# Folding two blocks of a random-feature projection at a time, each head on half the rows of TensorE's array

## The reference

```python
q = split_heads(x @ Wq.T + bq)          # 16 heads of 64
k = split_heads(x @ Wk.T + bk)
v = split_heads(x @ Wv.T + bv)
q_prime = relu(einsum('bhsd,hmd->bhsm', q, P)) / sqrt(64)   # P: 16 heads, 64 x 64
k_prime = relu(einsum('bhsd,hmd->bhsm', k, P)) / sqrt(64)
kv   = einsum('bhsm,bhsd->bhmd', k_prime, v)
attn = einsum('bhsm,bhmd->bhsd', q_prime, kv)
return attn @ Wo.T + bo
```

## Time and profile before

| | us |
|---|---|
| median of 3 runs | 1084.22 |
| lowest, highest | 1081.37, 1086.16 |
| the profiled execution | 1083.93 |
| its span | 1082.2 |
| TensorE products, busy | 1063.5 |
| TensorE weight loads, busy | 882.9 |
| VectorE, ScalarE, GpSimd, busy | 536.0, 289.8, 349.7 |

### The profile page before, as it was taken

The page is one execution under the profiler, slowest core; times in us unless marked ns, Lnnn a source line. Parts: engine busy times, 40 slices in busy tenths (PEclk is TensorE's granted clock), DMA queues, the critical chain, the costliest instruction groups (busy, mean ns, idle before and its releaser), DMA issues.

```text
span 1082.2 us, 15217 instructions
## 1 busy us (share of the span) xinstructions
PE 1063.5 (98%) x5527; PEld 882.9 (82%) x5527; DVE 536.0 (50%) x1152; ACT 289.8 (27%) x445; POOL 349.7 (32%) x225
## 2 busy tenths in 40 slices
PE   8999999999999999999969999999999999999998
PEld 7887778887878888888858888887788888888887
DVE  6944666676641222132427657967325212214684
ACT  5320211112222234132222223267222212202221
POOL 4000011122230024385400249955108744500151
PEclk9999999999999999999989999999999999999999
DMA  7303011222233387735594557766045556205912
GB/s 270 98 30 108 13 35 52 63 69 72 69 122 88 139 309 245 260 127 185 178 330 182 204 189 217 197 170 181 1 161 196 206 180 218 64 24 227 375 66 110
DMA packets 135933, 163.17 MB, mean 151 GB/s; under 512 B 8534, under 2 KB 102578, under 8 KB 130738
## 3 DMA queue, kind: packets, MB, share of 16 engines
q1 hardware_dynamic: 135282, 160.33, 44.8%
q10 hardware_dynamic: 576, 1.84, 0.4%
HBM read 107.70 MB, written 54.45 MB: 150 GB/s over the span
## 4 chain that ended last, share of the span: by engine, by line
PE 85%; DMA 5%; DVE 3%; POOL 3%; SPq 2%; ACT 1%; issue 1%; ACTq 0%; POOLq 0%
PE ps L2225 7%; PE ps L2227 7%; PE ps L2226 7%; PE ps L1890 6%; PE ps L1892 6%; PE ps L1891 6%; PE ps L2136 6%; PE ps L2138 6%; PE ps L2137 6%; PE ps L2159 4%; PE ps L2165 4%; PE ps L2056 3%; PE ps L2057 3%; PE ps L2058 3%; PE ps L1900 2%; PE ps L2002 2%
## 5 line engine op out<-in xcount | busy, mean ns | idle before, releaser
L1890 PE MATMUL ps<-w_hi,xnH 128*128 128x512 f32 x464 | 184.6, 398 | 0.0
L1892 PE MATMUL ps<-w_hi,xnL 128*128 128x512 f32 x464 | 180.9, 390 | 0.0
L1891 PE MATMUL ps<-w_lo,xnH 128*128 128x512 f32 x464 | 180.7, 389 | 0.0
L892 POOL TENSOR_TENSOR acc<-acc,cw 128x320 f32<-128x320 f32 x40 | 35.7, 893 | 252.6 <-ACT cw L1096 251.4
L1892 PEld LDWEIGHTS ps<-w_hi,xnL 128*128 128x128 f32 x464 | 87.1, 188 | 18.6
L1890 PEld LDWEIGHTS ps<-w_hi,xnH 128*128 128x128 f32 x464 | 87.1, 188 | 18.6
L1891 PEld LDWEIGHTS ps<-w_lo,xnH 128*128 128x128 f32 x464 | 87.2, 188 | 17.2
L1841 DVE TENSOR_TENSOR prd<-ps,wB 128x512 f32<-128x512 f32 (+1 forms) x24 | 14.2, 592 | 141.7 <-PE ps L2227 102.2
L2056 PE MATMUL ps<-xnH,w_hi 128*128 128x512 f32 (+1 forms) x192 | 68.1, 355 | 0.0
L2225 PE MATMUL ps<-x2H,guH 128*128 128x512 f32 (+1 forms) x192 | 67.7, 352 | 0.4 <-ACT wT L1334 0.4
L2226 PE MATMUL ps<-x2L,guH 128*128 128x512 f32 (+1 forms) x192 | 67.6, 352 | 0.0
(11 more groups left out here) (474 smaller groups left out, 2245.8 us busy)
## 6 DMA issues: line engine op xcount, KB each, us to landing
cR<-c_d SPq DMA_DIRECT2D x20, 640.0 KB, 4.8
foldin<-in SPq DMA_DIRECT2D x32, 256.0 KB, 2.8
guR<-in SPq DMA_DIRECT2D x16, 512.0 KB, 6.7
w_raw<-in SPq DMA_DIRECT2D x14, 512.0 KB, 6.6
c_d<-cw SPq DMA_DIRECT2D x40, 160.0 KB
wdq<-in SPq DMA_DIRECT2D x6, 1024.0 KB, 8.0
qR<-qT_d SPq DMA_DIRECT2D x20, 256.0 KB, 4.7
wd_d<-wd1H SPq DMA_DIRECT2D x5, 1024.0 KB, 5.4
```

The source lines that it names most:

```text
L1890: pe.matmul(target, xnH[:, kc, cols], wH[w][:, kc, :], start=(kc == 0), stop=False)
L1891: pe.matmul(target, xnH[:, kc, cols], wL[w][:, kc, :], start=False, stop=False)
L1892: mm = pe.matmul(target, xnL[:, kc, cols], wH[w][:, kc, :], start=False, stop=(kc == KC - 1))
```

## The change

Folds are made in pairs kc, kc + 1, in steps 2, 4, 6 and 8 of the stages (in the q stage after q jobs 1, 3, 5 and 7). A pair uses both `foldin` buffers. Each product takes one head: 64 rows of `foldin` (128 columns) against the 64 by 64 block of P without its zeros, at `tile_position=(a * HD, 0)`. The even heads (a = 0, rows 0 to 63) of both blocks go to the bank of the first job, the odd ones (rows 64 to 127) to the bank of the second. Even and odd products alternate. ScalarE and VectorE read a bank per job as before and put it, by head, in the two blocks' places of the panel. Both jobs are complete with the last products of the pair. `load_fold` and its place in SyncE's queue are as before.

```diff
+FOLD_AT = (2, 4, 6, 8)
@@ _job_ids
             names.append(("v", hf, t))
-            if 1 <= t <= KC:
-                names.append(("fold", hf, t - 1))
+            if t in FOLD_AT:
+                names += [("fold", hf, t - 2), ("fold", hf, t - 1)]
         for t in range(NT):
             names.append(("k", hf, t))
-            if hf == 1 and 1 <= t <= KC:
-                names.append(("fold", 2, t - 1))
+            if hf == 1 and t in FOLD_AT:
+                names += [("fold", 2, t - 2), ("fold", 2, t - 1)]
     for j in range(24):
         names.append(("q", j))
-        names.append(("fold", 3, j) if j < KC else ("m", (j - KC) // 2, (j - KC) % 2))
+        if j >= KC:
+            names.append(("m", (j - KC) // 2, (j - KC) % 2))
+        elif j % 2:
+            names += [("fold", 3, j - 1), ("fold", 3, j)]
@@
+        def by_heads(panel, kc):
+            rows = panel[:, kc - kc % 2:kc - kc % 2 + 2, :].rearrange("q k (g a m) -> q a k g m", g=4, a=2)
+            return rows[:, kc % 2]
+
+        def two_rows(target):
+            return target.rearrange("q (k g m) -> q k g m", k=2, g=4)
@@ fold_high
-                act.activation(wH[(1, 1, 0, 1)[f]][:, kc, :], job_bank(name), ACT.Copy).then_inc(fold_hi, 1)
+                act.activation(by_heads(wH[(1, 1, 0, 1)[f]], kc), two_rows(job_bank(name)), ACT.Copy).then_inc(fold_hi, 1)
@@ fold_low
-                dve.tensor_tensor(wL[w][:, kc, :], job_bank(name), wH[w][:, kc, :].bitcast(F32), ALU.subtract)\
+                dve.tensor_tensor(by_heads(wL[w], kc), two_rows(job_bank(name)), by_heads(wH[w], kc).bitcast(F32), ALU.subtract)\
                    .then_inc(ev, 1)
@@ ScalarE, VectorE and TensorE, each stage (the first shown)
-                if 1 <= t <= KC:
-                    fold_low(0, t - 1)
+                if t in FOLD_AT:
+                    for kc in (t - 2, t - 1):
+                        fold_low(0, kc)
...
-                if 1 <= t <= KC:
-                    fold(0, t - 1)
+                if t in FOLD_AT:
+                    fold(0, t - 2)
@@ fold on TensorE
-                name, n = ("fold", f, kc), fold_index(f, kc)
-                free_bank(name)
-                pe.wait_ge(in_fold[n % 2], 16 * (n // 2 + 1))
-                for g in range(4):
-                    mm = pe.matmul(job_bank(name)[:, g * P:(g + 1) * P], foldin[:, n % 2, g, :],
-                                   pbd_s[:, f % 2 * 4 + g, :], start=True, stop=True)
-                mm.then_inc(mm_done, 1)
+                names = (("fold", f, kc), ("fold", f, kc + 1))
+                for name in names:
+                    n = fold_index(f, name[2])
+                    free_bank(name)
+                    pe.wait_ge(in_fold[n % 2], 16 * (n // 2 + 1))
+                for k in range(2):
+                    for g in range(4):
+                        for a, name in enumerate(names):
+                            half = slice(a * HD, (a + 1) * HD)
+                            mm = pe.matmul(two_rows(job_bank(name))[:, k, g, :], foldin[half, k, g, :],
+                                           pbd_s[half, f % 2 * 4 + g, half], start=True, stop=True,
+                                           tile_position=(a * HD, 0))
+                            if k == 1 and g == 3:
+                                mm.then_inc(mm_done, 1)
```

More of the change, by code:

```diff
@@ L1087, in _ @@
                     act.activation(fbr[:], bank(5)[0:KC, P:2 * P], ACT.Copy).then_inc(bias_ev, 1)
-                if 1 <= t <= KC:
-                    fold_high(0, t - 1)
+                if t in FOLD_AT:
+                    for kc in (t - 2, t - 1):
+                        fold_high(0, kc)
             def window_out(w):
@@ L1106, in _ @@
                     panel_hi(0, t - 4, 2)
-                if s >= 2 * NT and 1 <= t <= KC:
-                    fold_high(s // NT - 1, t - 1)
+                if s >= 2 * NT and t in FOLD_AT:
+                    for kc in (t - 2, t - 1):
+                        fold_high(s // NT - 1, kc)
                 for w in WINDOWS.get(s, ()):
@@ L1153, in _ @@
                 q_feature(j)
-                if j < KC:
-                    fold_high(3, j)
-                else:
+                if j < KC and j % 2:
+                    for kc in (j - 1, j):
+                        fold_high(3, kc)
+                elif j >= KC:
                     g, h = (j - KC) // 2, (j - KC) % 2
@@ L1579, in _ @@
                     v_out(1, t)
-                if s >= 2 * NT and 1 <= t <= KC:
-                    fold_low(s // NT - 1, t - 1)
+                if s >= 2 * NT and t in FOLD_AT:
+                    for kc in (t - 2, t - 1):
+                        fold_low(s // NT - 1, kc)
             def m_low(g, h):
@@ L1594, in _ @@
             for j in range(24):
-                if j < KC:
-                    fold_low(3, j)
-                else:
+                if j < KC and j % 2:
+                    for kc in (j - 1, j):
+                        fold_low(3, kc)
+                elif j >= KC:
                     m_low((j - KC) // 2, (j - KC) % 2)
@@ L2038, in _ @@
                     rows(("v", hf, t), t, 0, ready=4 if t == 0 else None)
-                if s >= 2 * NT and 1 <= t <= KC:
-                    fold(s // NT - 1, t - 1)
+                if s >= 2 * NT and t in FOLD_AT:
+                    fold(s // NT - 1, t - 2)
                 for portion in PORTIONS.get(s, ()):
@@ L2085, in _ @@
                     degrees()
-                if j < KC:
-                    fold(3, j)
-                else:
+                if j < KC and j % 2:
+                    fold(3, j - 1)
+                elif j >= KC:
                     mixed((j - KC) // 2, (j - KC) % 2)
```

## The result

The changed kernel takes 1097.62 us (median; 1095.95 to 1100.98) where the kernel before takes 1085.00 beside it: a ratio of 1.0129 (95% interval 1.0114 to 1.0144), some 13 to 14 us slower. The forecast was +6.3 us, 1090.5. The direction was right and so was the price of the tiles, but the size was half of what came: more than half of the loss arose at a place where the prediction had put nothing. The profiled execution's span went from 1082.2 to 1095.7 us, +13.5.

What follows compares the result with a forecast made beforehand. TensorE's queue was taken to set the time. Steady part 0, tiling overhead 5.0, bank order 0.8 and x9's load 0.5 summed to +6.3 us, 1090.5 us against the median; own range 1087 to 1094, wider range 1083 to 1120.

Steps and rivals of the forecast that it cites:

- the price of the tiles: Sixteen fold pairs on TensorE: coming and going between tilings costs 0.29 or 0.35 us a pair, 5.0 us in all.
- The steady part is worth nothing: Fold pairs on TensorE: row halves load side by side, 1.79 us a pair, the same as two folds now.
- The serial rival: Fold pairs on TensorE: loads of the two row halves go one after another, 3.57 us a pair, 1117 us; chance 0.22.
- the half-load rival: Fold pairs on TensorE: a load of half the rows takes half the time or is hidden, 1077 us; chance 0.07.
- Sum: 10 x 0.29 + 6 x 0.35 = 5.0 us: Tiling-change overhead on TensorE: 0.29 us for ten pairs before float16 products (the windows), 0.35 for the other six.
- 0.8 is new: First stage, bank order: v3 waits for VectorE's eviction of v2 until 37.45, adding 0.8 us beyond the pairs' overhead.
- 0.5 us more: First stage, SyncE's queue: x9's load goes out late behind a fold load, so range_row on TensorE waits 0.5 us more.
- the first stage's forecast: Delay to the second product behind the first stage's last fold: 2.6 us more, including x9's 0.5.
- In the later stages the stores of the windows of odd steps stand behind a load_fold ... nothing: Later stages, SyncE: held window stores cost nothing, since ScalarE finds its cw buffer free before holding TensorE up.
- net 0.1, left out: ScalarE near 260 us: two odd steps lose a fold eviction, some 0.25 each; the even gains 0.6; net 0.1, uncounted.

Runs made afterwards that it cites:

- experiment 5: Changed kernel with a pair's products reordered, all even heads (rows 0 to 63) first, then all odd ones; 1126.44 us from one execution.
- experiment 2: Changed kernel's schedule of pairs, banks, loads and evictions, but with the old products of 128 rows by 128 columns; 1089.99 us, 1.0059 of the kernel before.
- experiment 1: Changed kernel with both fold loads of a pair issued in its even step (second v and k stages); 1091.53 us, 1.0064 of the kernel before.
- experiment 6: Changed kernel with the old 128 by 128 products and both fold loads of a pair issued in the even step; 1085.91 us, 1.0028 of the kernel before.
- experiment 10: Pairs of old full products, loads issued in the even step, but the first stage's eight folds one by one; 1083.50 us, 0.9993 of the kernel before.
- experiment 4: Changed kernel with each product cut again by weight columns into 64 x 64 tiles, 64 passes a pair; 1088.55 us, 1.0045 of the kernel before.
- experiment 3: Kernel before with window stores held in steps 1, 3 and 5 until the next step's fold is made; 1084.51 us, 1.0007 of the kernel before.
- experiment 12: Changed kernel (halves) with pair loads in even steps, x7 and x9 loads ahead, two steps' bounds loaded before the pair; 1091.31 us, 1.0056 of the kernel before.
- quarters: Changed kernel with 64 x 64 tiles: 1088.55 us; with even-step pair loads and x7, x9 ahead 1083.87; also with bounds loaded between rows and pair 1077.35.

## Why the prediction was half right

**"The steady part is worth nothing": right.** A pair takes 1.93 us with its overhead inside; the row halves load side by side (1.93 against 3.32 in experiment 5), and a load keeps its 128-column pitch of 0.104 to 0.106 us. The serial rival (3.57 a pair) and the half-load rival (0.93) both fell by the changed kernel's pairs; experiment 5 rules out what could still have given 1.93, loads of half the length one after another.

**"Sum: 10 x 0.29 + 6 x 0.35 = 5.0 us": about right.** The pair at 80.17 costs 0.35 more than two folds, and the q stage with its four grew by 1.5 (1.4 forecast). Ahead of the windows a pair costs 0.25 more than in experiment 2 (2.40 against 2.15 from the product ahead of it to the second behind), where 0.29 was forecast; all sixteen come to 4.6 us in the traces. By kernels that differ only in the tiles it was 3.9 us (experiments 1 and 6) and 7.6 (the changed kernel and experiment 2, both with a disturbed window stage, where a delay is not the tiles' alone).

**"0.8 is new", the order of banks: right in the trace, too small in time.** The product of v3 starts at 37.60, the transposes of cx at 52.42, 0.15 late and 0.08 early of the forecast. Experiments 6 and 10 price it: 3.0 to 3.8 us of time for the pairs of the first stage with products as before (0.0035 between the two, give or take 0.0014), more than the 1.5 by which the rows behind the stage's last fold start apart (81.42 against 79.96), a distance that is the same at the last q products. The rest of it wasn't found.

**"0.5 us more", x9: mechanism there, cost nothing.** x9 went out at 52.97 (forecast 52.9), but range_row didn't wait for it (the prediction's own 59.9 against 59.3 make 0.6, not 0.5). In experiment 4, whose pairs are shorter, it waited 0.9 us. Without this 0.5 the first stage's forecast is 2.1, as measured.

**"In the later stages the stores of the windows of odd steps stand behind a load_fold ... nothing": this step failed, together with the two evictions' "net 0.1, left out".** I asked only whether ScalarE finds a free cw buffer. That it does. What I didn't ask is what the held stores do when they go: with the two loads they make a burst, in which VectorE's register loads of the bounds go from 0.53 to 2.8 us, just when VectorE comes late from two evictions and TensorE, with no fold in the odd step, comes early to the windows. Each alone is free (experiments 3 and 6: stall 1.8 and 1.6 us); together they stall the windows by 5.3 us more in the changed kernel and bring a clock loss of 1.6. The prediction's sum had nothing for either, nor a term for the clock. Sending the pair's loads out together takes 0.0065 of the 0.0129 away (experiment 1), 7 us. That the step is this one is shown by experiments 1, 2, 3 and 6; that within "pairs" the lateness is made up of the eviction and the missing fold is read from traces only.

**Behind the q products** 1.0 us more was lost; TensorE's wait of 9.1 us for htmp is 11.2 after. It ranges from 8.1 to 11.6 over all kernels here without following their other losses; what sets it stays open.

**Open, too:** why the clock fell only in some executions. The profiles of experiments 1 and 12 show 3.4 us at half clock near 38 us, behind the wait for v2, which the changed kernel had as well (1.37 us) without a loss. The changed kernel's profile in turn shows 3.4 us at half clock near 9 us (0.53 from 9 to 12), before any fold, which the profile before doesn't have; TensorE's products stand up to 0.3 us later by it, a small part of the 2.1 in the table.

## What to carry to other kernels

Tiles smaller than the array pay only if they shorten what sets the pitch. Here that was the load of the weights' columns: halves of rows left it at 128 columns (nothing won, 0.25 to 0.35 us a pair lost), quarters made it 64 (0.5 to 0.6 us a pair won, coming and going included).

When a step is merged or moved, follow each queue to what it releases all at once, and ask who issues small latency-bound operations at that moment; register loads count among these, though no busy share shows them. Two edits that are each free can cost together: price them with the other one in place.

Shortening a stretch takes away a cover. The quarters won nothing until the loads of the bounds, hidden behind the old pair, were moved to where rows still run.

## What the hardware showed unasked

- Passes in the two row halves overlapped when they alternated in the queue and not when one half followed the other: 1.93 us a pair, and 3.32.
- Four 64 x 64 tiles in turn run at once: 64 passes of float32 in 1.09 us, 0.017 a pass.
- A register load of eight bytes takes 0.53 us by the median, and up to 3.0 us (3.1 in experiment 5) where a burst of transfers is under way.
- After a stretch in which TensorE was busy 2.28 of 4 us, the granted clock was 0.52 for 3.4 us (changed kernel, 268.0 to 271.4).
- VectorE's one-hots of 0.25 us took 0.75 and 0.90 beside an addition on GpSimd; all 29 of the changed kernel that took over 0.45 us overlapped with work of GpSimd, and 29 more did so and stayed short.
